# Mixture-of-experts kernel on one core: the low parts of the expert weights are computed per tile instead of kept for all experts

## The reference

```python
for e in range(8):      # W, V: [8, 128, 512]; W2: [8, 512, 128]
    h = silu(x @ W[e]) * (x @ V[e])
    y = y + gw[..., e:e + 1] * (h @ W2[e])
```

## Time and profile before

| what | us |
|---|---|
| median of three runs (1210.65 to 1218.12) | 1215.3 |
| the profiled execution | 1215.14 |
| its span in the trace | 1213.4 |
| PE busy | 1116.5 |
| DVE busy | 834.5 |
| ACT busy | 567.8 |
| POOL busy | 605.7 |

### The profile page before, as it was taken

How to read it: one execution, slowest core, us unless ns; L and a number is a source line. 1 busy time by engine, 2 the same in 40 slices (tenths; PEclk the granted TensorE clock), 3 DMA queues, 4 the chain that set the end, 5 groups by cost and what they waited for, 6 DMA issues and landing times.

```text
span 1213.4 us, 30866 instructions
## 1 busy us (share of the span) xinstructions
PE 1116.5 (92%) x9016; PEld 966.7 (80%) x9017; DVE 834.5 (69%) x3198; ACT 567.8 (47%) x1318; POOL 605.7 (50%) x666
## 2 busy tenths in 40 slices
PE   2699999999999999999999834999999999999994
PEld 1567777777777777777777634999999999999994
DVE  4447777777777777777766574777777777777773
ACT  2343534435435344354333423555555555555552
POOL 2001535353535353535353552666766666666664
PEclk9799999999999999999999966999999999999997
DMA  9251131130301311201010134444443444434442
GB/s 156 54 158 40 33 72 32 42 64 26 79 26 34 72 33 43 62 26 34 26 33 26 38 87 92 54 54 53 56 54 52 55 53 56 54 52 54 55 54 22
DMA packets 75795, 65.86 MB, mean 54 GB/s; under 512 B 12382, under 2 KB 66718, under 8 KB 75712
## 3 DMA queue, kind: packets, MB, share of 16 engines
q0 software_dynamic: 33024, 25.86, 15.2%
q1 hardware_dynamic: 42496, 38.59, 13.9%
q10 hardware_dynamic: 192, 0.37, 0.2%
HBM read 33.07 MB, written 31.71 MB: 53 GB/s over the span
## 4 chain that ended last, share of the span: by engine, by line
PE 86%; DVE 3%; issue 2%; SPq 1%; DMA 1%; ACT 1%; POOL 0%; POOLq 0%; DVEq 0%; ACTq 0%
PE bank L1243 21%; PE bank L1255 13%; PE bank L539 8%; PE bank L585 6%; PE bank L644 5%; PE bank L631 4%; PE bank L657 4%; PE bank L501 4%; PE bank L632 4%; PE bank L633 4%; PE bank L650 3%; DVE patches L748 2%; PE bank L425 2%; PE bank L532 2%; PE bank L1231 2%
## 5 line engine op out<-in xcount | busy, mean ns | idle before, releaser
L1384 POOL DMA_INDIRECT out_rows<-yo,dest x184 | 302.9, 1646 | 169.1 <-issue 116.4
L1243 PE MATMUL bank<-xT_e,wv 128*128 128x256 f32 x2208 | 289.9, 287 | 0.9 <-DVE xT_e L1335 0.9
L1243 PEld LDWEIGHTS bank<-xT_e,wv 128*128 128x128 f32 x2208 | 272.5, 190 | 1.4 <-DVE xT_e L1335 1.3
L1147 POOL DMA_INDIRECT sorted_rows<-xrow_all,sloti x192 | 188.8, 983 | 73.2 <-issue 54.8
L1313 ACT ACTIVATE sil<-bank 128x256 f32<-128x256 f32 x368 | 141.5, 384 | 160.5 <-PE bank L1243 156.7
L1342 DVE TENSOR_TENSOR hid<-sil,bank 128x256 f32<-128x256 f32 x368 | 154.8, 421 | 84.6 <-ACT sil L1313 74.2
L1255 PE MATMUL bank<-w,hid 128*128 x1472 | 179.5, 275 | 1.0 <-DVE hid L1342 1.0
L1120 POOL TENSOR_SCALAR vare<-mv 128x3 f32<-128x3 f32 x64 | 12.5, 195 | 324.1 <-issue 267.9
L1255 PEld LDWEIGHTS bank<-w,hid 128*128 128x128 f32 x1472 | 171.6, 192 | 1.2 <-issue 1.2
L1298 ACT CAST wv<-wv_all 128x1024 fp32r x92 | 96.5, 1049 | 41.0 <-issue 28.0
L1058 ACT ACTIVATE attn<-bank 128x256 f32<-128x256 f32 x128 | 49.4, 386 | 130.8 <-PE bank L633 130.8
(11 more groups left out here) (187 smaller groups left out, 1835.7 us busy)
## 6 DMA issues: line engine op xcount, KB each, us to landing
xr<-sorted_rows SPq DMA_DIRECT2D x92, 130.0 KB
raw<-in_x SPq DMA_DIRECT2D x64, 84.5 KB
raw<-in_x SPq DMA_DIRECT2D x60, 78.0 KB
out_rows<-attn SPq DMA_DIRECT2D x64, 58.5 KB
sorted_rows<-xrow_all,sloti POOLq DMA_INDIRECT x192, 2.4
out_rows<-yo,dest POOLq DMA_INDIRECT x184
wv_all<-in_L_ffn_W SPq DMA_DIRECT2D x8, 256.0 KB, 5.1
wv_all<-in_L_ffn_V SPq DMA_DIRECT2D x8, 256.0 KB, 5.2
```

Source lines behind the costliest of these rows:

```text
L1147: po.indirect_dma_start(sorted_rows, bass.IndirectOffsetOnAxis(sloti[:, p, j, ch:ch + 1], 0), xrow[:, p, j, ch], None).then_inc(s(f"scatte ...
L1243: q = pe.matmul(bank[fc][:, TT * m:TT * m + TT], wv[:, p, w_, m, cols], xT[:, p, x_], start=(w_ + x_ == 0), stop=(w_ == 1))
L1384: po.indirect_dma_start(out, bass.IndirectOffsetOnAxis(dest[:, p, a:a + 1], 0), yo[:, p, a], None, compute_op=ALU.add).then_inc(s(f"added{ ...
```

## The change

The low parts are no longer made in the drain, and the buffer `wl_all` is gone. DVE makes the low part of a tile's weights in that tile, by a subtraction of 1024 columns from `wv_all` and the rounded part in `wv`. It waits for that rounded part (`w_high`). ACT's rounding copy for tile t+1 moves from behind `copy_x` to the head of step t, ahead of silu 0 of tile t. Function `experts` no longer returns `lo_high` and `lo_low`, and their six calls in the drain go.

```diff
@@ function experts
-    wl_all = sb("wl_all", [128, E, 2, F])
...
-    PLACES_LOW = {(0, 1): (0, 2), (0, 2): (2, 4), (1, 0): (4, 6), (1, 1): (6, 8), (1, 2): (8, 10),
-                  (2, 0): (10, 12), (2, 1): (12, 14), (2, 2): (14, 16)}
-
-    def lo_high(ac, n, place):
-        for k in range(*PLACES_LOW.get((n, place), (0, 0))):
...
-            ac.copy(wv[:, k // 4 % 2, k // 2 % 2, k % 2], wv_all[:, k // 2, k % 2]).then_inc(s("lo_rounded"), 1)
-
-    def lo_low(ve, n, place):
...
-            ve.tensor_tensor(wl_all[:, k // 2, k % 2], wv_all[:, k // 2, k % 2],
-                             wv[:, k // 4 % 2, k // 2 % 2, k % 2].bitcast(F32), ALU.subtract).then_inc(s("lo_split"), 1)
@@ ACT
         def step(t, h, p, more, prev):
+            if more:
+                high_w(t + 1, 1 - p)
             for fc in range(4):
                 if more and fc == 2:
                     copy_x(t + 1, h + p, 1 - p)
-                    high_w(t + 1, 1 - p)
                 ac.wait_ge(s("hv_done"), 4 * t + fc + 1)
...
         ac.wait_ge(s("table_ready"), 2)
-        ac.wait_ge(s("lo_split"), 2 * E)
+        ac.wait_ge(s("weights_in"), 16 * 2 * E)
+        ac.wait_ge(s("conv_done"), NPAIR)
         high_w(0, 0)
@@ DVE
         def low_w(t, p):
             e = expert_of(ve, t)
+            ve.wait_ge(s("w_high"), t + 1)
             at_least(ve, s("hv_done"), 4 * (t - 1))
-            ve.tensor_copy(wv[:, p, 1].rearrange("p m n -> p (m n)"),
-                           wl_all[:, bass.ds(e, 1)].rearrange("p e m n -> p (e m n)")).then_inc(s("w_low"), 1)
+            ve.tensor_tensor(wv[:, p, 1].rearrange("p m n -> p (m n)"),
+                             wv_all[:, bass.ds(e, 1)].rearrange("p e m n -> p (e m n)"),
+                             wv[:, p, 0].rearrange("p m n -> p (m n)").bitcast(F32), ALU.subtract).then_inc(s("w_low"), 1)
...
         ve.wait_ge(s("table_ready"), 3)
-        ve.wait_ge(s("lo_split"), 2 * E)
+        ve.wait_ge(s("weights_in"), 16 * 2 * E)
         low_w(0, 0)
```

More of the change, by code:

```diff
@@ L284, in tokens @@
         met = (s("const_in"), 16)
-        expert_sync, expert_tensor, lo_high, expert_scalar, lo_low, expert_vector, expert_gpsimd = experts(
+        expert_sync, expert_tensor, expert_scalar, expert_vector, expert_gpsimd = experts(
             nc, ctx, s, met, ffw2, out, K, ident, table, wv_all, sorted_rows, bank)
@@ L798, in normalise @@
                                      ALU.mult).then_inc(s("qn_done"), 1)
-                if not a:
-                    lo_low(ve, n - NPAIR, 0)
                 if d:
@@ L839, in step @@
                     normalise(1)
-                if not a:
-                    lo_low(ve, n - NPAIR, 1)
                 front(0)
@@ L862, in step @@
                                      ).then_inc(s("xT_low"), 1)
-                if not a:
-                    lo_low(ve, n - NPAIR, 2)
                 if d:
@@ L1060, in q_exponent @@
                                   ACT.Exp).then_inc(s("q_exp"), 1)
-                if not a:
-                    lo_high(ac, n - NPAIR, 0)
                 if b:
@@ L1077, in step @@
                     image_norm(g + 1, 1)
-                if not a:
-                    lo_high(ac, n - NPAIR, 1)
                 if d:
@@ L1093, in step @@
                     image_norm(g + 1, 0)
-                if not a:
-                    lo_high(ac, n - NPAIR, 2)
                 if b:
@@ L1398, in gpsimd @@
             po.wait_ge(s(f"added{p}"), 16 * NT + 16)
-    return sync, tensor, lo_high, scalar, lo_low, vector, gpsimd
+    return sync, tensor, scalar, vector, gpsimd
 _INS = ["x", "L0_tok_gamma", "L0_tok_beta", "L0_tok_W", "L0_tok_b", "L0_attn_Wqkv", "L0_attn_Wout", "L0_attn_bout",
```

## The result

The changed kernel takes 1248.3 us (median of four runs, 1245.4 to 1249.8), the kernel before 1213.9 on the same chip (1210.7 to 1218.1). The ratio is 1.028, with a 95% interval of 1.024 to 1.032: 34.4 us slower, where 30 were forecast. The profiled execution of the changed kernel took 1245.4 us, the fastest of the four, and has a span of 1243.6 us.

The account below looks back on a forecast made before the run. The expert tiles were taken to be bound by PE, 4.89 us a tile. 1215.14 + 33.0 (waits at odd tiles) + 0.8 (the end) - 3.3 (drain) = 1245.6 us, given as 1245.5, range 1226 to 1262.

Parts of the forecast that it names:

- part 2: Steady tiles: ACT's copy ahead of the first silu delays `low_w`; block 0 of the next tile starts 0.75 us late.
- Part 1: DVE in each tile: subtraction of 1.22 us replaces a copy of 0.69, adding 0.52; alone it would be free.
- How often: Steady tiles: odd tiles wait and even ones don't, 44 odd tiles x 0.75 = 33.0 us.
- The products ahead of `down`: Steady tiles: products 2 and 3, which `down` waits for, come just in time, with a margin of 0.2 us.
- Part 3: Drain: all 16 pieces go from DVE, which gives back 3.3 us, bounds 2 and 5.
- what DVE gains behind it is lost: Drain from 715.70 on: the chain is SP's own queue up to the first load of rows, so DVE's gains don't count.
- Part 4: Ends: start hidden in the wait for rows; at the end tile 87's scale comes behind tile 89's `low_w`, adding 0.8 us.
- Case 2: Steady tiles: wait half as long, as ACT reads the number during silu 3 or the loop head costs less; 1228, chance 0.16.
- Case 3: Steady tiles: ACT's copy fits into its waits for PE, block 0 is never late, only the drain's gain remains; 1212, chance 0.09.
- Case 4: Steady tiles: subtractions and POOL's scatter-adds stretch each other, 1.52 us per subtraction, wait 1.05 us; 1259, chance 0.13.

Follow-up runs that it names:

- The kernel with the late copy: The changed kernel with ACT's rounding copy put back behind `copy_x`, subtraction per tile and empty drain kept; 1249.9 us, ratio 1.030.
- the kernel with the drain alone: The changed kernel with ACT's copy behind `copy_x` and DVE copying from `wv_all` instead of subtracting, so low parts aren't computed; 1210.0 us, ratio 0.996.
- the fastest kernel: The changed kernel with ACT rounding tile t+2 behind silu 3, its number read before silu 3, and DVE subtracting ahead of products 0 and 1; 1210.7 us.
- with four: The changed kernel with ACT's rounding copy back behind `copy_x` and four silu buffers instead of two; 1253.9 us, ratio 1.033.

## Why the prediction was right

**The forecast, 1245.5, and the result, 1248.3, agree in mechanism and place,** and no other case comes near: PE waits at block 0 of odd tiles and at no other place in the steady tiles, with DVE's `low_w` the last to arrive. The experiments show the three pieces of the chain in part 2: the branch and the reading of the expert's number ahead of ACT's copy (the copy at the tail, where neither lies ahead of it, 1215), the reading on DVE (moved into a wait, 1229), and the longer instruction (the early copy with the old copy of 0.69 us on DVE, 1226, with a wait of 0.25 instead of 0.86).

**Part 1, the subtraction.** 1.22 us was taken, 1.225 measured. The Trainium skill's (N + 151) / 0.96 (VectorE: DVE Perf Modes, the errata section) gives an estimate of 1224 ns, and this trace's 1224 to 1227 agree. The place behind `copy_x` was called free but for the further condition of the rounded part. That condition decides there: DVE waits 0.97 us for it, and the kernel is as slow as the changed one.

**Part 2, the wait at the odd tiles.** It is the term that was off: 0.84 us in the timeline shown, 0.86 in the mean, where I took 0.75, so 44 times it is 37.8 instead of 33.0. Part of it is not in the steps: they added up to 0.79, and 0.75 was taken. The step that was too short is ACT's way to the copy at the branch. I let the copy start 1.08 us after silu 3 (911.92 to 913.0), and it starts 1.17 after. The rest holds to a few hundredths: from the copy's start to the subtraction's 2.84 us, where I had 2.90, and 0.20 for PE's sequencer. With these, 1.17 + 2.84 + 1.23 + 0.20 = 5.44 from silu 3 to block 0 of the next tile, and PE could go on 911.99 - 907.39 = 4.60 after that silu, so 0.84.

**How often.** The even tiles have no wait, as told: their blocks 2, 3, 0, 1 are the unbroken runs at 905.67 and 916.28, since the wait of one tile covers what would be the next one's. The kernel with the late copy is the contrast. There the chain starts from block 1 of the tile itself, it closes on itself in every tile, and 0.43 us count 88 times.

**The products ahead of `down`** were called just in time, with a margin of 0.2; no wait of PE at L1242 shows in the steady tiles.

**Part 3, the drain.** 3.3 us was forecast, and it is what shows ahead of SP's queue: measured from the root, SP's first L381 piece starts at 34.22 us instead of 37.56, and at 34.20 in the kernel with the drain alone. More came in all: 4.5 by the chain of waits of the changed kernel, 3.9 by that of the kernel with the drain alone, and 5.1 by that kernel's median, whose interval takes in 3.3. The rest lies behind that point, where from SP's piece to the first expert matmuls are 28.2 us here, 28.8 with the drain alone and 29.4 before; the largest difference in it is the last padding DMA, 3.24 us here and 4.93 before. The kernel with ACT's early copy alone still has all 16 pieces, and its chain of waits is this:

```profile
676.86 0.90 POOL rstd L1122
...
714.37 0.81 SPq L381
...
734.47 3.58 DMA sorted_rows<-cst
...
742.75 2.93 PE bank L1243 x12
```

With the pieces, SP's piece is at 37.5 us from the root, as before, but the stretch behind it is 28.4 and the DMA 3.58 us, both no longer than with the drain alone (28.8 and 3.69). So that DMA varies between executions, and the bound "what DVE gains behind it is lost" has not been shown to fail. The 1.2 us above the forecast in the changed kernel's profile are not shown to be the pieces' doing.

**Part 4, the ends.** 0.8 was forecast and 0.4 measured. My own numbers, 0.33 and 0.4, add up to 0.7, and the scale's end did move by 0.72 against block 0 of tile 89 (0.33 ahead of it, then 0.39 behind); the tail from there was 0.3 us shorter. The scale of tile 87 ends behind block 0 of tile 89, as told.

**Case 2** (half the wait) is what the kernel with DVE's early reading shows at 0.44 us: 1229, where I gave 1228. It was the wrong engine: I had looked for the saving in ACT's sequencer. **Case 3** (nothing waits) isn't wrong about the engines. It needed the chain 0.8 us shorter, and with ACT's copy 0.9 us earlier behind silu 3 it comes out at 1215, with DVE's change as well at 1211 to 1212, where I gave 1212.

**Case 4** fell. The rows told that copies of 1024 columns go from 693 to 989 ns, and the Trainium skill (GPSIMD Engine Reference, Key points) says that POOL shares its SBUF interfaces with DVE and contends with instructions that have two SBUF inputs. With the copies' stretch this case took 1.52 us for each subtraction. None is longer than 1227 ns, in this kernel or in the fastest. The contention that the section tells of does show, but in POOL's instruction, as below.

**The sum with the measured terms**: 37.8 + 0.4 - 4.5 = 33.7 us, against 34.4 by the medians. The 4.5 is the drain of one pair of executions; with the 3.3 ahead of SP's queue it is 34.9. The forecast was 30.5 (33.0 + 0.8 - 3.3), so nearly all of its error is the 4.8 us of part 2.

## What to carry to other kernels

When an engine with idle time gets more work, follow the chain to the moment when the bound engine asks, with the branch, the reading of registers and each hand-off in it: here 0.1 us on it, at every second tile, is 4.4 us, and busy shares (DVE 72%, ACT 51%) say nothing of it. An instruction that depends on no recent result (ACT's rounding of weights) should go where its buffer comes free, a tile ahead, with its register read in a wait that exists anyway, rather than ahead of the first thing that others wait for. Where a loop hands from engine to engine, see whether the chain starts anew from the bound engine in each round or closes on itself, since that decides whether a wait counts once in two tiles or in all.

## What the runs showed of the hardware

**POOL pays when it starts under a subtraction.** In the timelines of POOL and DVE of the fastest kernel:

```profile
908.08 1.56 POOL L1359 DMA_INDIRECT out_rows<-yo,dest  x1 [0.92 <-issue]
909.94 2.51 POOL L1359 DMA_INDIRECT out_rows<-yo,dest  x1 [0.30 <-issue]
...
915.22 1.69 POOL L1359 DMA_INDIRECT out_rows<-yo,dest  x1 [0.30 <-issue]
```

```profile
909.80 1.23 DVE L1298 TENSOR_TENSOR wv<-wv_all,wv 128x1024 fp32r<-128x1024 f32 x1 [1.06 <-ACT wv L1264]
...
914.26 1.23 DVE L1298 TENSOR_TENSOR wv<-wv_all,wv 128x1024 fp32r<-128x1024 f32 x1 [0.69 <-PE bank L1230]
```

The scatter-add that starts at 909.94, with 1.09 us of the subtraction still to run, takes 0.95 us longer than its neighbour. The one at 915.22, with 0.27 us left to run, takes 0.13 longer. DVE's instruction has its 1.23 us each time. It is so all through the steady tiles of this kernel: the 78 scatter-adds that start under a subtraction take from 1.55 us with 0.01 left to run up to 2.58 with 1.16 left. In the changed kernel the scatter-adds start outside the subtractions (905.21 for 905.57, 915.83 for 916.18), and one that has already begun isn't lengthened: 1.55 us for the two named here. By the groups of instructions in the steady tiles, POOL's mean is 1792 ns in the fastest kernel and 1564 in the changed one, and the faster kernel has the slower POOL, since POOL isn't on the path.

**The name of a releaser can be wrong for a whole row of instructions.** ACT's silu was put down to DVE's product with two buffers (0.83 us) and with four (0.84), where that product can't hold it back. The experiment told that it was not the cause, and the first trace could have: silu 0 started 1.09 us after PE's block 0 (905.71 after 904.62), and in the kernel before, where no product is named, it is 1.08 (912.72 after 911.64). So it started when PE's block let it.
